# Selective scan of a four-part kernel: the sum over states for four of six channel tiles by a GpSimd product and by transposes that add up in PSUM, the products with B shared by GpSimd and ScalarE

## The reference, cut to what matters

```python
dt = softplus(dt @ dt_proj_w.T + dt_proj_b)
A = -exp(A_log)                                    # [768, 16]
def step(h_prev, inp):
    x_t, dt_t, B_t, C_t = inp                      # [768], [768], [16], [16] for each batch
    dA = exp(dt_t[..., None] * A)
    dBx = dt_t[..., None] * B_t[:, None, :] * x_t[..., None]
    h_new = dA * h_prev + dBx                      # [768, 16]
    y_t = einsum('bds,bs->bd', h_new, C_t)         # the sum over states
    return (h_new, y_t)
y = ys + xin * D
y = y * silu(z)
out = layernorm(y @ out_proj_w.T)
```

## Time and profile before

| | |
|---|---|
| median of 3 runs | 6409.91 us (6398.72 to 6418.82) |
| the profiled execution, its own time | 6409.13 us |
| its span, first to last instruction | 6407.5 us |
| mean granted TensorE clock | 0.933 |
| first scan starts, last scan starts | 127.5 us, 3850.2 us |

### The profile page before, as it was taken

How to read it: one execution, slowest core, us unless ns; L and a number is a source line. 1 busy time by engine, 2 the same in 40 slices (tenths; PEclk the granted TensorE clock), 3 DMA queues, 4 the chain that set the end, 5 groups by cost and what they waited for, 6 DMA issues and landing times.

```text
span 6407.5 us, 79336 instructions
## 1 busy us (share of the span) xinstructions
PE 5271.1 (82%) x29438; PEld 4117.7 (64%) x29438; DVE 4769.4 (74%) x6560; ACT 2723.1 (42%) x4651; POOL 2211.0 (35%) x2654
## 2 busy tenths in 40 slices
...
GB/s 65 1 19 19 8 8 8 8 23 16 8 8 8 8 27 12 8 8 9 15 8 8 5 34 5 30 10 36 5 35 11 14 44 28 30 23 30 30 30 19
DMA packets 71807, 115.89 MB, mean 18 GB/s; under 512 B 3926, under 2 KB 70002, under 8 KB 71422
## 3 DMA queue, kind: packets, MB, share of 16 engines
...
## 4 chain that ended last, share of the span: by engine, by line
PE 45%; DVE 30%; issue 16%; ACT 7%; POOL 1%; DMA 0%; SPq 0%; DVEq 0%; ACTq 0%; POOLq 0%
DVE a_h L710 13%; PE pw L1599 7%; DVE a_acc L724 7%; PE ps L1566 6%; PE pw L426 5%; PE ps L1047 4%; PE ps L337 3%; PE pw L1047 3%; PE ps L418 3%; DVE b_cv L1259 2%; PE ps L961 2%; ACT a_dA L551 2%; PE pw L1566 2%; PE ps L377 2%; DVE b_x L1357 1%
## 5 line engine op out<-in xcount | busy, mean ns | idle before, releaser
L710 DVE TENSOR_TENSOR_SCAN a_h<-a_dA,a_st,ps 128x384 f32<-128x384 f32 x1920 | 1866.6, 1001 | 78.3 <-PE ps L418 74.5
L551 ACT ACTIVATE a_dA<-a_dt,a_Aneg 128x384 f32<-128x384 f32 x2304 | 1324.4, 609 | 477.0 <-DVE a_h L710 471.0
L418 PEld LDWEIGHTS ps<-g_ident,a_dBT 128*128 128x128 f32 x6912 | 882.0, 146 | 733.2 <-DVE a_h L710 325.2
L814 POOL TENSOR_SCALAR a_dBT<-a_dtxT,a_BC 128x768 f32<-128x768 f32 x1152 | 1058.0, 935 | 821.6 <-PE ps L418 820.6
L418 PE MATMUL ps<-g_ident,a_dBT 128*128 128x128 f32 x6912 | 1186.1, 284 | 181.2 <-DVE a_h L710 171.4
L426 PE MATMUL pw<-g_ident,a_h 128*128 128x128 f32 x6912 | 1018.5, 288 | 123.3 <-DVE a_h L710 121.2
L724 DVE SCALAR_TENSOR_TENSOR a_acc<-pw,a_BC,a_acc 128x768 f32<-128x768 f32 x1080 | 1075.1, 996 | 29.3 <-PE pw L426 27.5
L426 PEld LDWEIGHTS pw<-g_ident,a_h 128*128 128x128 f32 x6912 | 830.8, 148 | 189.2 <-DVE a_h L710 179.9
L1707 DVE TENSOR_TENSOR d_hf<-d_hf,ps 128x384 f32<-128x384 f32 x288 | 159.2, 555 | 566.9 <-ACT d_hf L1637 556.3
L377 PE MATMUL ps<-a_xn,a_WinT 128*128 128x384 f32 x864 | 377.7, 523 | 91.9 <-DVE a_dt L615 41.2
L317 PE MATMUL ps<-a_WoT,a_sz 128*128 128x384 f32 x864 | 365.8, 508 | 80.1 <-ACT a_ob L438 74.5
...
## 6 DMA issues: line engine op xcount, KB each, us to landing
a_xs<-in_x SPq DMA_DIRECT2D x24, 576.0 KB, 3.9
x<-a_xs SPq DMA_DIRECT2D x24, 576.0 KB, 3.0
b_x<-x SPq DMA_DIRECT2D x24, 576.0 KB, 4.4
e_xs<-x SPq DMA_DIRECT2D x24, 576.0 KB, 3.9
out<-e_xs SPq DMA_DIRECT2D x24, 576.0 KB, 3.0
a_sx<-in_x SPq DMA_DIRECT2D x19, 576.0 KB, 4.0
...
```

What stands on the lines that cost most here:

```text
L418: t = e.transpose(m[f"ps{idx % 3}"][:, tb * 128:(tb + 1) * 128], m[f"a_dBT{g % 2}"][:, tb, c * 128:(c + 1) * 128], ident[:])
L551: e.activation(m[f"a_dA{idx % NDA}"][:], m[f"a_dt{k % 2}"][:, c, :], ACT.Exp, scale=m["a_Aneg"][:, c, n:n + 1]).then_inc(s["a_exp"], 1)
L710: e.tensor_tensor_scan(m[f"a_h{g % 2}"][:, c, :], m[f"a_dA{idx % NDA}"][:], m[f"ps{idx % 3}"][:, 0:T], 0.0 if q == 0 else m["a_st"][:, c, ...
L814: t = e.tensor_scalar(m[f"a_dBT{g % 2}"][:, tb, :], m[f"a_dtxT{o}"][:, tb, :], m[f"a_BC{o}"][:, tb, n:n + 1], 1.0, ALU.mult, ALU.mult)
```

## The change

**Sum over states.** For tiles 0 to 3 (`PT` = 4) GpSimd multiplies the state's `a_h`, in place, with C of that state, laid out along the positions and equal on all partitions (`a_cb`), one instruction of 128 x 1536. TensorE transposes the product into three PSUM banks, and each state's transposes add to what stands there; after the 16 states ScalarE copies the banks to `a_acc`, three instructions of 512 columns. Tiles 4 and 5 go the old way, by two transposes for each block of positions and a weighting on VectorE, now of 256 columns. The rows of C reach `a_cb` by DMA: ScalarE's `a_dtl` rows go to a DRAM tensor once a chunk (16 x 384), and come back spread over 128 partitions, two states at a time (128 x 768, three buffers, eight loads a chunk). The kept column is copied in two parts, before the product and at the end of the state.

**Products with B.** Of the three blocks of `a_dBT`, GpSimd makes the first, ScalarE the other two (its Copy with a scale), at steps 0 and 3 of the state before.

**Order.** `a_dA` has 10 buffers, filled 7 steps ahead. Tiles go in the order 4, 5, 0, 1, 2, 3 through projection, convolution and D term. Side work stands at other steps (below); the statistics of the next batch are read in three chunks, in the space of `a_ob`. The convolution on VectorE is of tiles 5 and 1.

```diff
-LEAD = 8
-NDA = 12
+LEAD = 7
+NDA = 10
+PT = 4
+PW = PT * 128
+DW = DI - PW
+NCB = 3
...
-A_AT = (0, 2, 3, 5, 6, 8)
-Z_AT = (53, 68, 71, 74, 80, 86)
+ORDER = (4, 5, 0, 1, 2, 3)
+A_AT = (6, 7, 11, 15, 19, 23)
+P_AT = (8, 12, 16, 20, 24, 27)
+Z_AT = (54, 69, 72, 75, 81, 87)
...
+def state_pe(e, m, w, g, c):
+    if g < 0:
+        return
+    s, ident, h = m.s, m["g_ident"], m[f"a_h{g % 2}"]
+    Y, D = state_banks(m)
+    if c in (1, 3):
+        w.wait_ge("v_scan", 6 * g + 6)
+        w.wait_ge("v_acc", 3 * g if c == 1 else 3 * g + 2)
+        for tb in ((0, 1) if c == 1 else (2,)):
+            for u in range(6 - PT):
+                at = DW * (tb % 2) + u * 128
+                t = e.transpose(D[:, at:at + 128], h[:, PT + u, tb * 128:(tb + 1) * 128], ident[:])
+            t.then_inc(s["pe_h"], 1)
+    if c >= 3:
+        tb, r = c - 3, g % NS
+        w.wait_ge("p_hc", g + 1)
+        if r == 0:
+            w.wait_ge("a_y", 3 * (g // NS))
+        for u in range(PT):
+            t = e.matmul(Y[tb][:, u * 128:(u + 1) * 128], h[:, u, tb * 128:(tb + 1) * 128], ident[:], start=r == 0 and u == 0, stop=r == NS - 1,
+                         is_transpose=True, skip_group_check=True)
+        if tb == 2:
+            t.then_inc(s["pe_y"], 1)
...
     for tb in range(TB):
-        yield 32 + 6 * tb
+        yield 5.1 + tb
+        w.wait_ge("pe_y", NS * (k + 1))
+        w.wait_ge("pe_A", 6 * k)
+        w.wait_ge("v_w", 2)
+        e.activation(m["a_acc"][:, tb, 0:PW], Y[tb], ACT.Copy).then_inc(s["a_y"], 1)
...
+    for tb in range(TB):
+        yield 35 + 6 * tb
         w.wait_ge("pe_O", 3 * k + tb + 1)
         w.wait_ge("pe_G", 3 * k)
         e.activation(m["a_ob"][:, tb, :], m["ps3"][:, 0:C], ACT.Copy).then_inc(s["a_ob"], 1)
-        yield 37.5 + 6 * tb
+        yield 40.5 + 6 * tb
...
-    yield 37
+    yield 40
     w.wait_ge("p_cv", 16 * (k + 1))
     w.wait_ge("v_cv", 8 * (k + 1))
     e.activation(m[f"a_xin{o}"][:], m[f"a_xin{o}"][:], ACT.Silu).then_inc(s["a_xi"], 1)
...
+        def main(n):
+            exp(STEPS * k + n + LEAD)
+            if n % 3 == 0:
+                scaled(NS * k + n // 6 + 1, 1 + n % 6 // 3)
...
+            if c < PT:
+                w.wait_ge("pe_y", g - 1)
+            else:
                 w.wait_ge("pe_h", 3 * (g - 1))
-                w.wait_ge("p_st", g - 1)
...
+def sum_dve(e, m, w, g, c):
+    if g < 0 or c not in (2, 4):
+        return
...
+        acc, ps, cs = m["a_acc"][:, tb, PW:DI], D[:, DW * (tb % 2):DW * (tb % 2) + DW], m[f"a_BC{k % 2}"][:, tb, 16 + r:17 + r]
...
+    def weighted(g):
+        h = m[f"a_h{g % 2}"]
+        w.wait_ge("v_scan", 6 * g + PT)
+        e.tensor_copy(m["a_st"][:, 0:PT, g % NS], h[:, 0:PT, T - 1]).then_inc(s["p_st"], 1)
+        w.wait_ge("p_st", 2 * g + 1)
+        w.wait_ge(f"d_cb{g // 2 % NCB}", 16 * (g // 2 // NCB + 1))
+        cb = m[f"a_cb{g // 2 % NCB}"][:, g % 2, :].unsqueeze(1).broadcast_to([128, PT, T])
+        e.tensor_tensor(h[:, 0:PT, :], h[:, 0:PT, :], cb, ALU.mult).then_inc(s["p_hc"], 1)
...
+            if c == 0:
+                scaled(g + 1)
+            if c == 1:
+                kept(g - 1)
+            if c == 4:
+                weighted(g)
...
+    def rows_in(p):
+        k, u = divmod(p, NS // 2)
+        if k < NCH:
+            w.wait_ge("d_cs", 16 * (k + 1))
+            w.wait_ge("p_hc", 2 * (p - NCB + 1))
+            e.dma_start(m[f"a_cb{p % NCB}"][:], d["cs"][k, 2 * u:2 * u + 2, :].partition_broadcast(128)).then_inc(s[f"d_cb{p % NCB}"], 16)
```

347 lines of the change are left out of this document (196 added, 151 removed).

## The result

| | before | after |
|---|---|---|
| median of 4 runs each | 6405.7 us (6398.7 to 6418.8) | 6487.3 us (6479.8 to 6501.3) |
| ratio, 95% interval | | 1.0127 [1.0101, 1.0154] |
| span of the profiled execution | 6407.5 us | 6477.8 us |
| last scan starts | 3850.2 us | 3937.1 us |

A forecast was written before the change was run, and what follows sets the result against it. VectorE was taken to bound the scans, 155.1 us a chunk. Less the weightings 129.7, then 1 + 10 + 5 - 1.5 gives 144.2; -10.9 times 24 is -262, +5 at the end, on 6409.1: 6152 us, range 6060 to 6260 (0.45).

The forecast's parts named there:

- the one on TensorE: TensorE's work in a state: 7.8 us against VectorE's 6.6 plus about 1 of layer norm, level, so nothing added.
- Removed from VectorE, 611 us: VectorE's weightings shrink from 768 to 256 columns, saving 25.4 us a chunk, 611 us in all.
- GpSimd, product with C 3.4 us: GpSimd's new 128 x 1536 product takes 3.4 us, a state 4.7; 1 us a chunk added for convolution states.
- the rival with 4.0: GpSimd's product with C costs 4.0 us: 148 a chunk, 6245 us; inside the forecast's own range, no separate chance.
- Contention, +10 us a chunk: VectorE's 14 two-input SBUF instructions wait for GpSimd's: three about 2.3 us, 11 0.3 each; range 0 to 28.
- Off by a factor of two: Named sign of failure: the VectorE-GpSimd contention's mean wait wrong by a factor of two (10 us a chunk, 240 us).
- SiLU block, +5 us: Behind ScalarE's SiLUs, VectorE stalls 5.3 us a chunk where it lost 0.3: 11.2 us to cover with 5.8.
- Chunk boundary, -1.5 us: At chunk boundaries the six a_acc transposes no longer follow each other: 1.5 us a chunk saved, estimated from 6.3 idle.
- DMAs, nothing: Eight loads of 384 KB and one small store a chunk on SP's queue come in time: nothing added.
- Slower: VectorE and GpSimd take turns: Rival: all 14 two-input VectorE instructions wait 2.0 us on the mean, 28 a chunk, 6584 us; slower 0.13, nearly all this.
- ScalarE holds TensorE at further places: Rival: softplus and gate copies in ScalarE's queue stall too; two more stalls give 6392 us, one 6272; chance 0.15.
- More arrives: Rival: half the contention and no SiLU stall, 133.2 us a chunk, 5888 us; chance 0.22 for under 6060.

The follow-up runs named there:

- run 1: The changed kernel with TensorE's second group of old-way transposes moved from step 3 to step 5 of a state; 6179.5 us, 0.9631 of before.
- run 2: The changed kernel with VectorE's first two weightings of a state after tile 1's scan instead of tile 2's; 6177.0 us, 0.9625 of before.
- run 4: The kernel before with one wait tightened: state transposes wait for the weighting just ahead, as if pw had one buffer; 6510.2 us, 1.0145 of before.
- run 6: On top of run 2, VectorE's convolution and dt instructions and GpSimd's dt*x moved to steps meant to miss the product with C; 6097.4 us, 0.9497 of before.
- run 7: The changed kernel with the moves of run 1, run 2 and run 6 together; 6081.7 us, 0.9476 of before.
- run 8: Run 7 with ScalarE's SiLU pair one place later, behind the copy a_ob<-ps; 6096.4 us, 0.9501 of before.
- run 3: The changed kernel with the moves of run 1 and run 2 together; 6144.0 us, 0.9575 of before.

## Why the prediction was wrong

**The step that failed** is the one on TensorE: "As many transposes of states as before ... level, so I add nothing". It counted TensorE's instructions and not what they wait for: it took busy time, level with VectorE's, and set the wait at nothing. The price of the omitted wait is 308 us by run 1 and 310 by run 2, 12.9 us a chunk, against a forecast gain of 257. It was there to be read before: the diff has `v_acc >= 3g + 2` at step 3 and `sum_dve` at `c == 2`, and the earlier trace rows have every duration of the loop. From the end of the weightings, with the queue full, TensorE needs two transposes, four transposes, one matmul and three transposes, 0.22 + 0.44 + 0.64 + 0.33 = 1.6 us, and VectorE offers one scan, 0.91. 0.7 us in each of 384 states is 270 us, an estimate that the 279 us ahead of tile 4's scan bear out, and nothing in the sum held it. The condition "as long as the others keep up" was tested by sums of busy time alone, never by the order in which an engine meets its waits.

The Trainium skill, Perfetto Trace Analysis, section Matmuls, has the rule that this breaks: independent groups of matmuls should go round several PSUM banks, so that the evacuation of one overlaps the next. The trace agrees, with a limit: waiting as if there were no second buffer cost 93 us in before (run 4), and in after the 310 us went away with the one bank still in use (runs 1 and 2), so what counted was what stood behind the wait.

Point by point:

- **Removed from VectorE, 611 us.** Right. The mean of a weighting went from 996 to 463 ns, x1152 that is 614 us. VectorE's busy time fell by less, 460; 71 us of the difference are longer instructions of the convolution and dt (below), and 70 are overlap that is gone: the durations of VectorE's instructions in the stretch add up to 323 us more than its busy time before and to 253 more after, since neighbours no longer overlap where VectorE waits between them.
- **GpSimd, product with C 3.4 us.** Right: 3.46, so the rival with 4.0 is out. In after it bounds nothing: TensorE waits 0.4 us in all for it (L466), and GpSimd itself idles 1101 us in front of `a_st` for the scans. Once the kernel is faster, VectorE does wait for GpSimd's queue: 36.8 us at L656 in run 2.
- **Contention, +10 us a chunk.** The mechanism is right, the size too high by two or three. The three groups of after

```profile
L691 DVE SCALAR_TENSOR_TENSOR a_dt<-a_raw,a_dt 128x384 f32<-128x384 f32 x144 | 135.3, 942 | 19.3 <-ACT a_dt L560 19.3
L682 DVE SCALAR_TENSOR_TENSOR a_xin<-a_raw,a_pv,a_xin 128x384 f32<-128x384 f32 x144 | 122.6, 851 | 0.2
...
L679 DVE TENSOR_SCALAR a_xin<-a_raw,a_pv 128x384 f32<-128x384 f32 x48 | 39.0, 814 | 13.8 <-ACT a_raw L507 13.8
```

  have 296.9 us (busy us, mean ns, idle before), in before 225.5 (means of 594, 793 and 542): 71.4 us, 3.0 a chunk. In run 2, where VectorE is less held, it is 338.1, so 4.7 a chunk, and moving the instructions (run 6) won 3.3. Of the three instructions that I let fall into a product and wait 2.3 us each, two do, at steps 17 and 71: over 1.6 us in 23 and 20 of 24 chunks, with means of 2.10 and 1.81, so 1.5 and 1.3 us more than alone. The third, at step 23, misses it (mean 0.52); it is a first tap, with one tensor input, and I had counted it and its like as having two. The other 11, counted at 0.3 each, 3.3 together, were in part counted twice: the chunk of before already holds 1.9 us of such waits, by the means of the three groups against their shortest. "Off by a factor of two" was named as a way to fail; it was, to the good side.
- **SiLU block, +5 us.** ScalarE's sum was near: 113 us a chunk where 119 were counted. The cause is right and the size about half in after: the same place of a chunk shows 2.70 us in front of L648 and 0.33 in front of the scan, 3.0 in all, since VectorE came to it already late. With TensorE's wait gone it is the 5.1 us of run 7, in one chunk. The reading "from the release to the scan" did not tell that a copy in ScalarE's queue is what counts, wherever it stands; run 8 did.
- **Chunk boundary, -1.5 us.** Wrong sign. The D term's wait for `ps L323` rose from 21.1 us in before (there in front of L571) to 119.8; 17.2 are left with both moves (run 3), so it was mostly the same wait's work. That the six transposes gain by standing apart shows in no run.
- **DMAs, nothing.** Right; 384 KB of C rows land in 3.4 us and no engine's list over the scans' stretch has a wait for them.
- **The rivals.** "Slower: VectorE and GpSimd take turns" had the sign but not the mechanism: the contention was 3.0 us a chunk and not 28. "ScalarE holds TensorE at further places" has little in the rows: `a_ob`'s copies 74.7 us, no other of ScalarE's over 30. "More arrives" has no run on its side: run 7, with every move, still stands at 6082 and not at 5888. The forecast itself is nearly what runs 1 to 3 gave (6180, 6177, 6144) with the wait taken out. That 6144 lies 8 us from 6152 is luck: there VectorE idles 13.7 us a chunk, where the sum had 9.8, and the contention is 6.1, where the sum had 10; the two errors of 3.9 cancel. None of the signs of failure that I named was this wait.
